# Tokens' 192 values as 128 and 64 rows in place of 96 and 96, the 64 rows of two outputs on the two halves of the array

## The chip, the cores and the metric

The program runs on one core of one Trainium2 chip, as one launch. The metric is the device time of that launch in microseconds (us). TensorE multiplies and transposes, VectorE (DVE), ScalarE (ACT) and GpSimd (POOL) work on what it leaves in the banks of PSUM, and SyncE (SP) issues most transfers. All data is float32.

## What is computed

The reference embeds 16 images (25 patches each) and 16 texts (77 words each) as 102 tokens of 192 values a sample, and passes them through four layers, each an attention and a feed-forward part with a normalisation ahead. The parts that matter here are these (the others, layer 0 and the two mixtures of experts, stay as they are):

```python
# layer 1, attention part: gated convolution, attention with 12 heads of 16, MLP
x = x + _ssm(_ln(x, ln1_g, ln1_b), in_proj_w, conv_w, conv_b, out_proj_w)      # x @ (192, 768)
a = _attn(_ln(x, ln2_g, ln2_b), qkv_w, qkv_b, H)                               # x @ (192, 576)
x = x + a @ attn_proj_w + attn_proj_b
h = jax.nn.gelu(_ln(x, ln3_g, ln3_b) @ ffn1_w + ffn1_b, approximate=False)     # x @ (192, 768)
x = x + h @ ffn2_w + ffn2_b
# layer 2: attention with 12 heads of 64, then an MLP
q = _split_heads(x @ w_q); k = _split_heads(x @ w_k); v = _split_heads(x @ w_v)  # each (192, 768)
h = jax.nn.gelu(jnp.einsum('td,hd->th', xt, in_weight) + in_bias, approximate=False)
# layer 3: attention without softmax, with a decay mask
qkv = x @ W_qkv + b_qkv                                                          # (192, 576)
```

Each product with x sums over its 192 values. An array of 128 rows does that in two steps.

## The kernel before

The 16 samples are worked on in four groups (NG) of four samples (GB): 408 tokens (TG) a group. Each engine has its own program, one `@block` each, and its order is the order in which the code is written. Semaphores tie the programs together. PSUM has eight banks: SBANKS are 0 and 1, TBANKS 2 and 3, OBANKS 4 and 5, XBANKS 6 and 7, FBANKS 2, 3, 6 and 7. In TensorE's program `claim` (L1541) waits until a bank is free, `filled` says that it is full, and `moved` waits until what is in it has been taken.

Six stages of layers 1 to 3 work alike, each in a loop over the four groups: the convolution (L1899), attention 1, MLP 1, attention 2, MLP 2 and attention 3. A group goes so:

1. DVE and POOL normalise the tokens into XN (token rows, 192 columns).
2. `xt` (L1590) turns XN with transposes at L1579: values 0 to 95 of the 408 tokens into one XBANK, values 96 to 191 into the other, each transpose a matmul with the identity of 102 columns. ACT copies both into XT, 96 rows by 2 parts (`turned`, L1330; L1338 with scale and bias in layer 1, L1336 without). TensorE waits for both copies.
3. `product` (L1557; its matmuls all bear L1561) makes each block of 128 outputs by 408 tokens in one bank from two matmuls over 96 rows each. There are 6 blocks in the convolution (first halves of the pairs to DVE, L1062 to L1066; second to ACT, L1470), 6 in attention 1 (q and k, ACT L1477 and L1484), 6 in an MLP (ACT L1345), 12 in attention 2 (ACT L1508 to L1513) and 4 blocks of 96 in attention 3. q and k use XBANKS alternately.
4. The values V are made with the tokens as rows: 102 by 192 for each sample in attention 1 and 3, two blocks of 102 by 384 for each sample in attention 2 (16 samples in all). DVE moves them out of OBANKS (L882, L885).
5. An attention stage then runs `attention`: scores (L1651) into SBANKS and bank 6, from which DVE takes the extremes (L847), ACT the exponentials (L1382), POOL the scaling (L620), TensorE the transposes (L1690) and the products with V (L1680), and the projection (L1663). An MLP makes its second product at L1627.

A float32 matmul is two records in the trace, each with its own load of weights. So a block of step 3 is 4 records, and 24 records are six blocks.

The mixtures of experts already have another layout: `first` (in `experts`) does two blocks with 128 rows each (L1993), and then the remaining 64 rows of both on the two halves of the array's rows (L1995).

SP loads the weights of layer 1 into AREA once layer 0 no longer reads it, with 22 transfers (W1_LOADS); POOL waits for them, spreads the weights of q and k into 32-row heads (L665), and gives `padded`, for which DVE waits at L1043 before its first normalisation of the stage. Those of layers 2 and 3 come with 15 transfers (W2_LOADS), ahead of the store of rows (L512) for the first mixture of experts.

## Time and profile before

| | us |
|---|---|
| median of 3 runs | 1974.52 |
| lowest and highest | 1970.76, 1977.46 |
| the profiled execution's own time | 1975.56 |
| its span, first to last instruction | 1973.8 |

The profile is of that one execution. It lists every instruction with its engine, line and tile, and tells for each idle time what ended it. A row of the timeline merges neighbours of one kind: start, length, how many (x), and in brackets how long the engine was idle before, and what ended that. The length reaches to the end of the last matmul's result, which lies after the start of the next row, so paces are taken here from start to start. The granted clock of TensorE is 1.00 at 2.4 GHz and 0.50 at 1.2 GHz.

### The profile page before, as it was taken

The numbers are of one execution on the slowest core, as the hardware profiler recorded it, in microseconds if no ns is written. First come the engines' busy times: TensorE is split into PE (matmuls) and PEld (weight loads), VectorE is DVE, ScalarE is ACT, GpSimd is POOL, SyncE is SP. The second block draws the span as 40 slices with busy tenths as digits, with TensorE's granted clock in tenths as the row PEclk, the third lists the DMA queues.
The fourth block names the chain that finished last, engine by engine and source line by source line (L and its number), as shares of the span: only waits on it lengthen the run. The fifth ranks groups of instructions, "written<-read, shape, count | busy, mean of one in ns | idle before, by whom it ended". The sixth has DMA issues, their size and how long they took to land.

```text
span 1973.8 us, 30712 instructions
## 1 busy us (share of the span) xinstructions
PE 1555.4 (79%) x9952; PEld 1118.0 (57%) x9952; DVE 746.1 (38%) x2156; ACT 653.9 (33%) x1667; POOL 382.8 (19%) x450
## 2 busy tenths in 40 slices
PE   7978788845554577788889589868999899789993
PEld 4555554634222244555567478736656677678883
DVE  1254535562111027655552612236543523531112
ACT  0455455511000013366653111124543532203331
POOL 5120211210000002222220135402211200023330
PEclk9587867766767678899999579979999999659997
DMA  7132141332999980000000535310000200134543
GB/s 191 31 92 81 40 121 31 91 97 67 273 286 283 285 248 31 1 1 0 0 0 0 152 108 175 118 39 1 0 0 0 96 0 0 34 94 149 161 139 87
DMA packets 85962, 177.79 MB, mean 90 GB/s; under 512 B 34602, under 2 KB 53200, under 8 KB 83832
## 3 DMA queue, kind: packets, MB, share of 16 engines
q1 hardware_dynamic: 71344, 127.50, 23.4%
q10 hardware_dynamic: 7392, 33.03, 5.7%
q0 software_dynamic: 7136, 16.10, 2.7%
q8 instruction: 51, 0.84, 0.2%
q14 instruction: 39, 0.32, 0.1%
HBM read 149.61 MB, written 26.99 MB: 89 GB/s over the span
## 4 chain that ended last, share of the span: by engine, by line
PE 51%; issue 16%; DMA 14%; DVE 14%; ACT 3%; POOL 1%; another core or an unknown queue 1%; SPq 0%; DVEq 0%; POOLq 0%; ACTq 0%
PE bank L1561 13%; DMA AREA<-in_fc 10%; PE bank L2005 6%; PE bank L1993 5%; PE bank L1995 4%; PE bank L1752 3%; PE bank L1663 3%; DVE MXU L847 3%; PE bank L1744 3%; DVE SMU L853 3%; PE bank L1651 2%; PE bank L1680 2%; PE bank L1806 2%; PE bank L1690 2%; PE bank L1961 1%
## 5 line engine op out<-in xcount | busy, mean ns | idle before, releaser
L1561 PE MATMUL bank<-XT,AREA 96*128 96x408 f32 (+1 forms) x640 | 241.2, 536 | 33.0 <-ACT XT L1338 15.7
L1561 PEld LDWEIGHTS bank<-XT,AREA 96*128 96x128 f32 (+1 forms) x640 | 122.6, 197 | 140.5 <-issue 101.4
L1651 PE MATMUL bank<-KZ,QT 128*102 128x102 f32 x1152 | 148.2, 271 | 6.9 <-ACT PB L1382 3.6
L620 POOL TENSOR_TENSOR PB<-PB,RCU 102x306 f32<-102x306 f32 x96 | 66.8, 696 | 390.4 <-DVE RCU L854 390.4
L1651 PEld LDWEIGHTS bank<-KZ,QT 128*102 128x102 f32 x1152 | 129.5, 184 | 22.3 <-issue 13.7
L606 POOL TENSOR_TENSOR RS<-VE,expo 102x4 f32<-102x4 f32 (+1 forms) x53 | 53.0, 1000 | 445.4 <-DVE VE L792 389.5
L2005 PE MATMUL bank<-WM,KZ 128*128 x660 | 120.4, 331 | 0.0
L1993 PE MATMUL bank<-KZ,SLOTS 128*128 128x128 f32 x660 | 116.0, 300 | 2.5 <-issue 2.5
L1663 PE MATMUL bank<-AREA,OT 128*102 128x192 f32 x384 | 89.8, 347 | 32.1 <-DVE SLOTS L1079 11.2
L1680 PE MATMUL bank<-PT,V 102*32 102x102 f32 (+1 forms) x1152 | 87.1, 274 | 28.2 <-DVE OT L868 28.2
L2005 PEld LDWEIGHTS bank<-WM,KZ 128*128 128x128 f32 x660 | 108.2, 194 | 0.4
L1993 PEld LDWEIGHTS bank<-KZ,SLOTS 128*128 128x128 f32 x660 | 93.4, 198 | 16.6 <-issue 5.3
L715 POOL DMA_INDIRECT rows_out<-KZ,TARGET x66 | 66.6, 1010 | 172.8 <-DVE KZ L1216 136.0
L1752 PE MATMUL bank<-AREA 64*102 64x203 f32 x384 | 86.5, 500 | 16.7 <-ACT SLOTS L1418 7.2
L1376 ACT ACTIVATE PT<-bank 102x306 f32<-102x306 f32 x192 | 81.4, 425 | 44.9 <-PE bank L1690 43.8
L1363 ACT ACTIVATE KZ<-bank,AREA 128x128 f32<-128x128 f32 x198 | 54.6, 374 | 119.1 <-PE bank L1995 62.0
L1209 DVE COPY KZ<-bank 128x256 f32<-128x256 f32 x66 | 28.0, 424 | 169.0 <-PE bank L1981 117.8
L1451 ACT ACTIVATE QT<-bank 128x512 f32<-128x512 f32 (+1 forms) x32 | 15.7, 490 | 221.5 <-PE bank L1806 221.5
L620 POOL TENSOR_TENSOR ON<-ON,RCU 102x306 f32<-102x306 f32 x96 | 66.8, 696 | 109.4 <-DVE RCU L854 109.4
L1995 PE MATMUL bank<-KZ,SLOTS 64*128 64x128 f32 x660 | 84.3, 333 | 0.0
L1017 DVE COPY QT<-bank 128x192 f32<-128x192 f32 x16 | 5.7, 358 | 206.6 <-PE bank L1806 206.6
L1752 PEld LDWEIGHTS bank<-AREA 64*102 64x102 f32 x384 | 60.5, 242 | 39.8 <-ACT SLOTS L1418 10.2
(292 smaller groups left out, 2722.4 us busy)
## 6 DMA issues: line engine op xcount, KB each, us to landing
WM<-in_fc SPq DMA_DIRECT2D x9, 2304.0 KB, 22.2
AREA<-in_fc SPq DMA_DIRECT2D x9, 2304.0 KB, 17.7
WM<-in_fc ACTq DMA_DIRECT2D x7, 2304.0 KB, 29.1
AREA<-in_fc ACTq DMA_DIRECT2D x7, 2304.0 KB, 28.3
SLOTS<-in_m3w SPq DMA_DIRECT2D x33, 384.0 KB
SLOTS<-in_m1w SPq DMA_DIRECT2D x33, 256.0 KB
AREA<-pos_scratch SPq DMA_DIRECT2D x16, 459.0 KB
pos_scratch<-AREA SPq DMA_DIRECT2D x8, 913.5 KB
```

The costliest lines, as they stand in the source:

```text
L620: pool.tensor_tensor(p, p, scale, ALU.mult).then_inc(sem["probs_ready"], 1)
L715: pool.indirect_dma_start(rows_out, bass.IndirectOffsetOnAxis(ap=TARGET[:, i:i + 1], axis=0), YO[i % YRING], None, bounds_check=2 * NB * T ...
L847: give(dve.tensor_reduce(MXU[:, n % 4, 0:HPU], scores, AX.X, ALU.min), "probs_in")
L1376: free(activation(PT[s % 2][:, 0:HPU, :], src, ACT.Copy), k)
L1561: last = pe.matmul(dst, lhsT, rhs, start=n == 0, stop=n == len(pieces) - 1)
L1651: last = pe.matmul(psum[k][0:T, cols(j)], QT[:, tile, cols(bb)], KALL[:, unit % per_tile * (HEADS // per_tile) + tile, cols(bb)], start=Tr ...
L1663: last = pe.matmul(psum[PROJBANK][0:T, 0:D], OT[bb % 2][:, m, :], wo[:, m, :], start=m == 0, stop=m == parts - 1)
L1680: last = pe.matmul(psum[k][row:row + rows, cols(tile)], by_head(dv)[:, bb * HEADS + h, :], PT[n % 2][:, j, :], start=True, stop=True)
L1752: last = pe.matmul(p[0:T, j * NREL:(j + 1) * NREL], head(QR, h, 2, 64, cols(bb)), head(RT, h, 2, 64, slice(0, NREL)), start=True, stop=True)
L1993: pe.matmul(p[:, c], w_all[:, (j * per + m) * 128:(j * per + m + 1) * 128], x[:, 0:TILE], start=True, stop=False)
L1995: both = [pe.matmul(p[:, c], w_half[64 * j:64 * j + 64, c], x[64 * j:64 * j + 64, TILE:2 * TILE], start=False, stop=True) for j, (k, p) in ...
L2005: last = pe.matmul(p[:, 0:D], HG[i % HRING][:, f * 128:(f + 1) * 128], w2[:, bass.ds(e, 1), f * D:(f + 1) * D].rearrange("p o d -> p (o d) ...
```

## The change

XT becomes XT2, 128 rows by 2 parts. Part 0 holds values 0 to 127. Part 1 holds values 128 to 191 twice: in rows 0 to 63 and again in rows 64 to 127. Weights are loaded accordingly: rows 0 to 127 of each matrix in one tile, and in a second tile (`...h`) rows 128 to 191 of every first output in partitions 0 to 63 and of every second output in partitions 64 to 127. The products of two outputs are made together (`twin`): two matmuls over 128 rows into two banks, then two over 64 rows, one on each half of the array's rows. `columns_twice` does so for blocks of outputs, `rows_twice` and a loop in attention 2 for V. The router's products keep the layout of 96 and 96 (XT is the first 96 rows of the same tile).

```diff
-W1_LOADS = 6 + 8 + 8
-W2_LOADS = 8 + 7
+W1_LOADS = 2 * 3 + 5 + 3 + 6 + 8 + 8
+W2_LOADS = 4 * 3 + 5 + 3 + 7
...
-        XT = sb("XT", [KD, 2, TG])
+        XT2 = sb("XT", [128, 2, TG])
+        XT = XT2[0:KD]
...
+            def load_split(full, half, src, name, columns):
+
+                load(full, t[src][0:128], name)
+                for j in range(2):
+                    load(half[64 * j:64 * j + 64], columns(t[src][128:D], j), name)
...
             step(pool.memset(wqk1, 0.0))
+            step(pool.memset(wqk1h, 0.0))
             pool.wait_ge(sem["w1_loaded"], 16 * W1_LOADS)
...
+            for full, _ in (g1, b1):
+                step(pool.tensor_copy(full[KD:128, :, 0], full[KD:128, :, 1]))
...
             with at.loop(act, NG) as g:
-                turned(XT, g1[:, 1, :], b1[:, 1, :])
-                for dst in range(3):
-                    k = at.bank(XBANKS)
-                    free(activation(QT[:, dst, :], full(k)[:, 0:TG], ACT.Identity, scale=-0.25,
-                                    bias=bqk1[:, dst:dst + 1]), k)
+                turned_split([g[:, 1, :] for g in g1], [b[:, 1, :] for b in b1])
                 for j in range(3):
-                    k = at.bank(XBANKS)
+                    k = at.bank(FBANKS)
+                    free(activation(QT[:, j, :], full(k)[:, 0:TG], ACT.Identity, scale=-0.25,
+                                    bias=bqk1[:, j:j + 1]), k)
+                    k = at.bank(FBANKS)
                     src = full(k)[:, 0:TG]
...
+            def xt_split(x=XN):
...
+                for part in range(2):
+                    k, p = claim(XBANKS)
+                    for bb in range(GB):
+                        if part == 0:
+                            last = pe.transpose(p[:, cols(bb)], x[:, bb, 0:128], ident[0:T, 0:T])
+                            continue
+                        pe.matmul(p[64:128, cols(bb)], x[:, bb, 128:D], ident[0:T, 0:T], start=True, stop=True)
+                        last = pe.transpose(p[0:64, cols(bb)], x[:, bb, 128:D], ident[0:T, 0:T])
+                    out.append(filled(last, k))
...
+            def twin(dsts, full, half):
+
+                for j, dst in enumerate(dsts):
+                    say_taken(pe.matmul(dst, *full(j), start=True, stop=False))
+                return [pe.matmul(dst, *half(j, slice(64 * j, 64 * j + 64)), start=False, stop=True)
+                        for j, dst in enumerate(dsts)]
...
-                for dst in range(6):
-                    k, p = claim(XBANKS)
-                    qk.append(filled(product(p[:, 0:TG], two(wqk1, dst * 128, (dst + 1) * 128)), k))
-                v_moved = pairs(lambda bb: token_rows(XT, bb, wqkv1, 2 * D, 3 * D))
-                moved(*qk[-2:])
+                qk = columns_twice(6, wqk1, wqk1h, apart=HPU)
+                v_moved = rows_twice(wqkv1[:, 2 * D:3 * D], wqkv1h[:, D:2 * D])
+                moved(*qk[-4:])
...
                 for bb in range(GB):
-                    for c in range(0, FF, 2 * D):
-                        k, p = claim(OBANKS)
-                        v_moved.append(filled(product(p[0:T, 0:2 * D], token_rows(XT, bb, wv2, c, c + 2 * D)), k))
-                moved(*qk[-2:])
-                attention(2, 64, wo2, v_moved[-2:])
+                    claims = [claim((OBANKS, SBANKS)[bb % 2]) for _ in range(2)]
+                    lasts = twin([p[0:T, 0:2 * D] for k, p in claims],
+                                 lambda j: (XT2[:, 0, cols(bb)], wv2[:, 2 * j * D:2 * (j + 1) * D]),
+                                 lambda j, r: (XT2[r, 1, cols(bb)], wv2h[r]))
+                    v_moved += [filled(last, k) for last, (k, p) in zip(lasts, claims)]
+                moved(*qk[-4:])
+                attention(2, 64, wo2, v_moved[-4:])
```

TensorE's order in one group of MLP 1, before. XN is the normalised input, AREA holds weights, KZ the hidden values; a size is output rows by columns.

```order
L1579 MATMUL bank6<-ident,XN 96x102 x4
L1544 REGISTER_ALU
L1579 MATMUL bank7<-ident,XN 96x102 x4
L1555 REGISTER_ALU
L1544 REGISTER_ALU
L1561 MATMUL bank2<-XT,AREA 128x408 x2
L1544 REGISTER_ALU
L1561 MATMUL bank3<-XT,AREA 128x408 x2
L1561 MATMUL bank6<-XT,AREA 128x408 x2
L1561 MATMUL bank7<-XT,AREA 128x408 x2
```

The same place now, to the end of the second pair of blocks.

```order
L1644 MATMUL bank6<-ident,XN 128x102 x4
L1590 REGISTER_ALU
L1646 MATMUL bank7<-ident,XN 64x102
L1647 MATMUL bank7<-ident,XN 64x102
...
L1655 MATMUL bank2<-XT,AREA 128x408
L1655 MATMUL bank3<-XT,AREA 128x408
L1656 MATMUL bank2<-XT,AREA 128x408
L1656 MATMUL bank3<-XT,AREA 128x408
L1655 MATMUL bank6<-XT,AREA 128x408
L1655 MATMUL bank7<-XT,AREA 128x408
L1656 MATMUL bank6<-XT,AREA 128x408
L1656 MATMUL bank7<-XT,AREA 128x408
```

The second part of XT takes eight matmuls (L1646 and L1647, four times each) in place of four, and each pair of banks is filled by four matmuls (L1655 over 128 rows, L1656 over 64 rows) whose last two end together.

TensorE's order where attention 2 goes from V to the scores, now (before, V used banks 4 and 5 alone and each bank was filled by two matmuls in a row).

```order
L1655 MATMUL bank0<-AREA,XT 102x384
L1655 MATMUL bank1<-AREA,XT 102x384
L1656 MATMUL bank0<-AREA,XT 102x384
L1656 MATMUL bank1<-AREA,XT 102x384
L1601 REGISTER_ALU x3
L1732 REGISTER_ALU
L1737 MATMUL bank0<-KZ,QT 102x102 x3
```

The last V of a group now lies in banks 0 and 1, and the first scores go into bank 0, so they wait until DVE has taken V out of it.

SP's order at the loads of layer 1, before and then now: 22 transfers up to `in_qk_b`, then 36.

```order
L414 DMA AREA<-in_in_proj 96x2x768
L414 DMA AREA<-in_out_proj 128x3x192
L414 DMA AREA<-in_qkv 96x2x576
L414 DMA AREA<-in_proj 128x576
L414 DMA AREA<-in_ffn 96x2x768
```

```order
L416 DMA AREA<-in_in_proj 128x768
L416 DMA AREA<-in_in_proj 64x384 x2
L416 DMA AREA<-in_qkv 128x576
L416 DMA AREA<-in_qkv 64x192 x4
L416 DMA AREA<-in_ffn 128x768
L416 DMA AREA<-in_ffn 64x3x128 x2
```

Each matrix of 192 rows is now three transfers or more in place of one.

## Rows read from the trace of the kernel before

**Rows 1.** The page, part 4: the chain that ended last, by engine.

```profile
PE 51%; issue 16%; DMA 14%; DVE 14%; ACT 3%; POOL 1%; another core or an unknown queue 1%; SPq 0%; DVEq 0%; POOLq 0%; ACTq 0%
```

**Rows 2.** Stretches (convolution, attention 2): length, busy us and counts, clock, DMA.

```profile
745.00:824.00 79.00, 61.21 (x224) 40.56 (x224) 55.32 (x142) 27.84 (x40) 24.46 (x21) 0.86 0.00 1
...
1302.00:1565.00 263.00, 241.85 (x1499) 165.02 (x1498) 130.71 (x332) 120.74 (x340) 48.58 (x68) 0.99 0.00 0
```

**Rows 3.** Timeline, TensorE, one group of MLP 2 (granted clock 1.00).

```profile
1584.65 8.48 PE L1561 MATMUL bank<-XT,AREA 96*128 96x408 f32 x24 [0.83 <-ACT XT L1336]
1592.97 8.00 PE L1627 MATMUL bank<-AREA,KZ 128*102 128x192 f32 x48
1600.81 0.86 PE L1579 MATMUL bank<-ident,XN 102*96 102x102 f32 x8
```

**Rows 4.** Timeline, TensorE: the experts' pairs, and layer 0's heads on half the rows.

```profile
1884.61 0.71 PE L1993 MATMUL bank<-KZ,SLOTS 128*128 128x128 f32 x4
1885.26 0.49 PE L1995 MATMUL bank<-KZ,SLOTS 64*128 64x128 f32 x4
1885.68 0.71 PE L1993 MATMUL bank<-KZ,SLOTS 128*128 128x128 f32 x4
...
192.07 0.94 PE L1752 MATMUL bank<-AREA 64*102 64x203 f32 x8
```

**Rows 5.** Timeline, TensorE, attention 2: three heads of 64 columns.

```profile
1339.23 0.56 PE L1680 MATMUL bank<-PT,V 102*64 102x102 f32 x6
```

**Rows 6.** Timeline, ACT: the copies into XT, in MLP 2 and in MLP 1.

```profile
1583.51 0.90 ACT L1336 ACTIVATE XT<-bank 96x408 f32<-96x408 f32 x2 [6.29 <-PE bank L1579]
...
1031.60 1.26 ACT L1338 ACTIVATE XT<-bank,AREA 96x408 f32<-96x408 f32 x2 [6.29 <-PE bank L1579]
```

**Rows 7.** Timeline, attention 2 from V to the scores: TensorE, then DVE.

```profile
1322.69 10.48 PE L1561 MATMUL bank<-AREA,XT 96*102 96x384 f32 x32
1333.01 1.78 PE L1651 MATMUL bank<-KZ,QT 128*102 128x102 f32 x18
...
1333.28 0.56 DVE L882 COPY V<-bank 102x384 f32<-102x384 f32 x1 [0.73 <-PE bank L1561]
1333.96 1.07 DVE L847 TENSOR_REDUCE MXU<-bank 102x3 f32<-102x306 f32 x2
```

**Rows 8.** Timeline, attention 1, the second group: TensorE, ACT, then DVE.

```profile
877.08 7.09 PE L1561 MATMUL bank<-XT,AREA 96*128 96x408 f32 x20 [1.05 <-ACT XT L1338]
...
886.77 2.77 PE L1561 MATMUL bank<-AREA,XT 96*102 96x192 f32 x16
890.20 1.83 PE L1651 MATMUL bank<-KZ,QT 128*102 128x102 f32 x18 [0.67 <-issue]
...
882.83 7.26 ACT L1484 ACTIVATE KZ<-bank,AREA 32x408 f32<-32x408 f32 x12 [0.77 <-PE bank L1561]
...
890.99 1.07 DVE L847 TENSOR_REDUCE MXU<-bank 102x3 f32<-102x306 f32 x2 [0.80 <-PE bank L1651]
```

**Rows 9.** Timeline, the convolution's third group: TensorE, then DVE.

```profile
791.63 5.80 PE L1561 MATMUL bank<-XT,AREA 96*128 96x408 f32 x8 [3.99 <-DVE marked L761]
...
794.76 0.70 DVE L1062 TENSOR_SCALAR KZ<-bank,AREA 128x408 f32<-128x408 f32 x1 [0.57 <-PE bank L1561]
```

**Rows 10.** Timeline, the loads of layer 1: SP, POOL and DVE.

```profile
720.26 0.32 SPq L414 DMA_DIRECT2D AREA<-in_in_proj  x1
...
730.22 4.04 SPq L414 DMA_DIRECT2D AREA<-in_qk_b  x8
...
736.24 1.23 POOL L665 COPY AREA<-AREA 96x192 f32<-96x192 f32 x4 [14.64 <-DMA AREA<-in_qk_b]
...
740.00 0.17 DVE L1043 TENSOR_SCALAR AREA<-AREA 128x3 f32<-128x3 f32 x1
```

**Rows 11.** Timeline, SP: the store of rows, and its next issue.

```profile
1101.51 8.48 SPq L512 DMA_DIRECT2D rows_in<-V  x16
1123.88 0.37 SPq L526 DMA_DIRECT2D SLOTS<-in_m1w  x1
```

More of the change, by code:

```diff
@@ L315, in build @@
         a2(KD, 2, NB * T)
-        wq2, wk2, wv2 = a2(KD, 2, FF), a2(KD, 2, FF), a2(KD, 2, FF)
+        wq2, wk2, wv2, wi2 = (a2(128, FF) for _ in range(4))
+        wq2h, wk2h, wv2h, wi2h = (a2(128, FF // 2) for _ in range(4))
         wo2, bo2 = a2(128, 6, D), a2(T, D)
-        wi2, bi2, wu2 = a2(KD, 2, FF), a2(128, FT), a2(128, FT, D)
-        wqkv3, bqk3, bv3 = a2(KD, 2, 3 * D), a2(KD, 4), a2(T, D)
+        bi2, wu2 = a2(128, FT), a2(128, FT, D)
+        wqkv3, wqkv3h, bqk3, bv3 = a2(128, 3 * D), a2(128, 2 * D), a2(KD, 4), a2(T, D)
         decay = a2(T, T)
@@ L877, in values @@
                 v5 = by_head(dv)
-                for first in range(0, GB * HEADS, per):
-                    k = at.bank(OBANKS)
+                for n, first in enumerate(range(0, GB * HEADS, per)):
+                    k = at.bank((OBANKS, SBANKS)[n // 2 % 2])
                     src = full(k)[0:T, 0:per * dv].rearrange("p (h d) -> p h d", d=dv)
@@ L1339, in turned, with turned_split @@
                                         bias=bias[:, part:part + 1]), k)
+            def turned_split(scale=None, bias=None):
+                for part in range(2):
+                    k = at.bank(XBANKS)
+                    src = full(k)[:, 0:TG]
+                    if scale is None:
+                        free(activation(XT2[:, part, :], src, ACT.Copy), k)
+                    else:
+                        free(activation(XT2[:, part, :], src, ACT.Identity, scale=scale[part][:, part:part + 1],
+                                        bias=bias[part][:, part:part + 1]), k)
             def hidden(tiles, func, bias, src_ready=None):
@@ L1612, in pairs, with mlp @@
                 return out
-            def mlp(tiles, w1, x, w2):
-                tokens = []
-                for m in range(tiles):
-                    k, p = claim(FBANKS)
-                    last = product(p[:, 0:TG], [(w1[:, part, m * 128:(m + 1) * 128], x(part)) for part in range(2)])
-                    tokens.append(filled(last, k))
+            def mlp(tiles, w1, w2):
+                tokens = columns_twice(tiles, *w1)
                 for first in range(0, GB, 2):
@@ L1900, in convolution_in @@
                 at.first_banks()
-                xt()
+                xt_split()
                 for c in range(CT3):
-                    k, p = claim(SBANKS)
-                    filled(product(p[:, 0:TG], two(win1, c * 128, (c + 1) * 128)), k)
-                    k, p = claim(TBANKS)
-                    filled(product(p[:, 0:TG], two(win1, INNER + c * 128, INNER + (c + 1) * 128)), k)
+                    at_c = c * 128
+                    claims = claim(SBANKS), claim(TBANKS)
+                    lasts = twin([p[:, 0:TG] for k, p in claims],
+                                 lambda j: (win1[:, j * INNER + at_c:j * INNER + at_c + 128], XT2[:, 0, :]),
+                                 lambda j, r: (win1h[r, at_c:at_c + 128], XT2[r, 1, :]))
+                    for last, (k, p) in zip(lasts, claims):
+                        filled(last, k)
             def convolution_out(place):
```

123 lines of the change are left out of this document (80 added, 43 removed).

## The prediction

> **What bounds the kernel now.** I read the chain that ended last first: TensorE has 51% of it, and 16% is time in which TensorE waits for nothing that the profile shows [rows 1]. The stretches come next, one for each stage. Attention 2 has TensorE busy for 242 of 263 us at a granted clock of 0.99, while in the convolution it is busy for 61 of 79 us, beside DVE's 55, at 0.86 [rows 2]. So TensorE's time is the time of the kernel in the dense stages, and in the convolution it is so only in part. The timeline of a dense stage shows how full: one group of MLP 2 runs from transposes to transposes with a single wait, 0.83 us for the copies into XT [rows 3].
>
> **A price for a matmul.** 24 records of 408 columns take 8.32 us from start to start (1584.65 to 1592.97), of which the first load of weights is about 0.1; that leaves 0.342 us a record. 48 records of 192 columns take 7.84 us, 0.163 each [rows 3]. Both are 0.85 ns a column, whether 96 or 128 rows are used. V of attention 2, 384 columns, has 0.322 us (10.32 / 32) [rows 7]. So rows cost nothing and records do: a pair of blocks is now 8 records, 8 x 0.342 = 2.74 us.
>
> **Do the halves run at once, and what does going to halves cost?** The experts' pairs show it. One unit there is four records over 128 rows and four over 64 rows, and repeats after 1.07 us (1884.61 to 1885.68) [rows 4]. At 0.85 ns a column, 128 columns are 0.109 us; eight in a row would be 0.87 and six (the halves at once) 0.65. That the halves do overlap is shown by the other row: eight records of 203 columns on half the rows, four into one bank and four into the next, take 0.94 us with everything that follows the last one [rows 4], where eight in a row would be 8 x 0.173 = 1.38 us before that. So the unit is 6 x 0.109 plus two changes between whole and halved rows, and a change costs (1.07 - 0.65) / 2 = 0.21 us: the array runs empty, and the next load of weights lies bare.
>
> A pair of blocks then costs 6 x 0.342 + 2 x 0.21 = 2.47 us, **0.27 less than now**. More than half of the two saved records (0.68) goes back in changes. For V: 8 x 0.322 = 2.58 becomes 6 x 0.322 + 0.38 (102 columns load faster, so 0.19 a change) = 2.31, 0.27 less for a sample of attention 2; 8 x 0.163 = 1.30 becomes 0.98 + 0.38 = 1.36, 0.06 more for two samples of attention 1 and 3.
>
> **XT.** The second part takes eight matmuls for four, those of rows 64 to 127 as plain matmuls of two records. On two column halves they can overlap: three heads of 64 columns, two of them on one half, take 0.56 us for six records [rows 5]. A record of 102 columns is 0.087, and the last result needs 0.16 to come out (1584.65 + 8.48 is 0.16 past the next start [rows 3]), so 0.56 is a load of 0.05, four records in a row (0.35) and 0.16; six in a row would be 0.73. So part 1 is 8 x 0.087 = 0.70, a change of 0.15 (64 columns load in half the time) and 0.08 for the wider part 0, against 0.35 now: its bank is full 0.58 us later. ACT's copies hide a part. Without bias the second copy starts 0.40 after the first (0.90 for both), and its bank is full just before; 0.5 is late. With bias it starts 0.6 later (1.26 for both) [rows 6], so 0.31 is late. Were the eight to run in a row (12 records), it would be 0.34 more each.
>
> **Stage by stage**, four groups each:
> - MLP 1: 3 pairs save 0.81, XT adds 0.31: -2.0 us. MLP 2: 0.81 less 0.5: -1.2. Cover for the last pair, whose banks are now full together: ACT takes 0.6 us for 408 columns (7.26 / 12 [rows 8]), and TensorE wants them after 8 and 10 records of 0.163, 1.3 and 1.6 us on; enough.
> - Attention 2: 6 pairs save 1.62, V saves 1.06, XT adds 0.5. A wait is added: the first scores go into bank 0, which holds V until DVE has copied it. Now DVE starts on the first scores (L847) at 1333.96, 0.95 after the last V record (1333.01) [rows 7]; its own last copy ends only then. In the changed order DVE starts a copy 0.27 after V's end, as now (1333.28), frees bank 0 after 0.56 more, the six records take 0.1 to be released, 0.09 to load and 6 x 0.09, and DVE is there 0.25 after: 1.8 after V's end. That is 0.85 later, and behind it stand the exponentials, POOL and all else, since TensorE waits for them at once. Net -1.33 a group: -5.3 us.
> - Attention 1 is bound by ACT at this point. Its twelve copies of k run without a gap from 882.83 for 7.26 us, and the scores start when they end (890.20), 13.0 after the first product (877.2); DVE at 890.99 [rows 8]. The changed order alternates q and k, so ACT has a k to copy after the first pair: 2.42 + 3 x (0.6 + 2.43) = 11.6 after the first product. TensorE's pairs and V (3 x 2.47 + 0.5 for a bank + 2 x 1.36 = 10.6) and DVE's two moves of V after them (0.6 each, to 12.0) stay below DVE's new start of 12.4. So the stall shrinks by 1.36, XT adds 0.31: -4.2 us.
> - Attention 3: two pairs save 0.54, V adds 0.12, XT 0.5: +0.3.
> - Convolution: TensorE waits 3.99 for DVE, then DVE 0.57 for TensorE at block 5 [rows 9]. DVE's block used to be full after 4 records, and is now full after the whole pair. At full clock that is 0.9 us later (2.26 for 1.37), cold 1.8. I followed the four groups: +1.5 in the first (cold), the third gives back what TensorE saves, the last ends about 2 later. I take +2, from -1 to +5.
> - Loads of layer 1: 36 for 22. The eight small ones are issued every 0.46 us (4.04 / 8 with the first longer), the 22 take 14.1 us to 734.3, of which 10.1 is issuing and 3.9 waits on full queues. 36 x 0.46 = 16.6, up to 20.5 with the same waits: 2.5 to 6.5 later. DVE starts at 740.00, 2.5 us after POOL's copies end (737.47) [rows 10]. POOL's own work grows by 0.25. So 0.2 to 4.2 is late; I take 1.5. Layers 2 and 3: 12 more loads stand ahead of the store of rows, +5.5 us; SP sits idle from 1109.98 to 1123.88 after it [rows 11], so nothing.
>
> The **sum**: -2.0 - 1.2 - 5.3 - 4.2 + 0.3 + 2 + 1.5 = -8.9 us. The profiled execution took 1975.6, so 1966.7; that execution lies 1.0 above the median of 1974.5, hence 1965.6, rounded to 1966.
>
> **Rivals.**
> 1. A change costs more behind 408 columns than behind 128. There are 160 changes in the pairs and 64 in V, 224 in all; each 0.04 us more eats the gain, and at 0.28 in place of 0.21 the time is 1966 + 16 = 1982, **slower than before**. It decides at 0.25. For it: a 408-column record runs on for 0.16 us after its last column, and nothing shows a change right behind one in a full-clock stretch. Against: the experts' 128-column records run on as long, and their change does not wait for it.
> 2. The halves do not overlap in this order (both records of one, then both of the other), so that a pair has seven record times. This adds 80 x 0.342 and 16 x 0.163 + 16 x 0.322, 35 us: about 2001. Against it stands the 0.94 us row of [rows 4], which has this very order.
>    [...]
> 3. XT's part 1 runs in a row (24 x 0.34 = +8), or the convolution and the loads come out at their upper ends (+3, +2.7): 1972 to 1977, no change to be told.
> 4. The waits hide less than I think: the scores of attention 2 start earlier, and the convolution and loads cost nothing (-3.4, -2, -1.5): 1959. It is inside the forecast's sign.
>
> **How the numbers follow.** About 0.3% (5.9 us) is what a measurement of this kernel can tell from no change. The forecast with rival 4 (1957 to 1971): 0.67, of which 0.05 lies within 0.3%. Rival 3: 0.19, nearly all within. Rival 1: 0.10, of which 0.02 within. Rival 2: 0.04. That is faster 0.62, same 0.25, slower 0.13. The range leaves out rival 2, the worse half of rival 1 and the best tail: 1955 to 1978.
>
> **What would show it.** In the trace after: pairs that repeat every 2.47 us in MLP 2, with the halves of two banks starting within 0.02 us of each other; a group of MLP 2 of 17.5 us for 17.85; the first DVE extreme of attention 2 1.8 us after V; q and k copies of attention 1 alternating, the scores at 11.6 us; the first L1043 at 740.2 to 744 us. Wrong would be: a pair above 2.74 us, a granted clock that falls in the dense stages because the changes leave TensorE idle, or part 1 of XT above 1.1 us.

## The result, and the profile after

The changed kernel takes **1999.55 us** (median of 4 runs, 1988.78 to 2011.26), the kernel before 1972.64 us (median of 4, 1969.08 to 1977.46). The ratio is 1.0136, with a 95% interval from 1.0073 to 1.0199: slower, where the forecast was 1966 us and faster. The profiled execution took 2002.3 us with a span of 2000.3; before, the span was 1973.8. All rows below are of these two executions unless another kernel is named.

The chain that ended last looks as before [rows 1], a little more of it in `issue` (the page, part 4, of the changed kernel):

```profile
PE 49%; issue 17%; DVE 14%; DMA 13%; ACT 4%; SPq 1%; POOL 1%; DVEq 0%; POOLq 0%; ACTq 0%
```

The place to look at is one group of MLP 2, the stage whose group had a single wait before [rows 3]. Timeline of TensorE, changed kernel (start, duration, engine, line, output<-inputs, count, idle time before). L1644 makes part 0 of XT; L1646 (matmuls to rows 64:128) and L1647 (transposes to rows 0:64) make part 1; L1655 are the products over 128 rows (whole), L1656 those over 64 rows (halves); L1713 is the MLP's second product:

```profile
1593.96 0.51 PE L1644 MATMUL bank<-ident,XN 102*128 102x102 f32 x4
1594.41 0.39 PE L1646 MATMUL bank<-ident,XN 102*64 102x102 f32 x2
1594.73 0.28 PE L1647 MATMUL bank<-ident,XN 102*64 102x102 f32 x1
1594.93 0.39 PE L1646 MATMUL bank<-ident,XN 102*64 102x102 f32 x2
...
1596.31 0.28 PE L1647 MATMUL bank<-ident,XN 102*64 102x102 f32 x1
1597.49 2.68 PE L1655 MATMUL bank<-XT,AREA 128*128 128x408 f32 x4 [0.90 <-ACT XT L1383]
1600.10 1.55 PE L1656 MATMUL bank<-XT,AREA 64*128 64x408 f32 x4
1601.58 1.64 PE L1655 MATMUL bank<-XT,AREA 128*128 128x408 f32 x4
1603.15 0.96 PE L1656 MATMUL bank<-XT,AREA 64*128 64x408 f32 x4
1604.03 1.64 PE L1655 MATMUL bank<-XT,AREA 128*128 128x408 f32 x4
...
1606.49 8.09 PE L1713 MATMUL bank<-AREA,KZ 128*102 128x192 f32 x48
```

Three things stand there. The second pair starts at 1601.58 and the third at 1604.03: **2.45 us a pair**, as the prediction has it (2.47). XT takes from 1593.96 to 1596.58, **2.62 us where it was 0.86** [rows 3], because matmuls and transposes of 64 columns take turns, one couple for each sample ("to and fro" from here on), 0.52 us a couple (1594.41 to 1594.93). And the first pair takes 4.09 us (1597.49 to 1601.58), not 2.45. The stretches of the same group say why (length, then busy us and counts of PE, PE's loads, DVE, ACT, POOL, then the granted clock, DMA share and GB/s):

```profile
1593.90:1596.60 2.70, 2.69 (x18) 1.55 (x16) 1.76 (x6) 0.51 (x1) 0.00 (x0) 1.00 0.00 0
1597.40:1601.50 4.10, 4.01 (x8) 1.47 (x8) 1.25 (x4) 1.03 (x1) 1.01 (x1) 0.58 0.00 0
1601.60:1606.40 4.80, 4.80 (x18) 1.94 (x16) 0.00 (x0) 2.18 (x4) 0.00 (x0) 1.00 0.00 0
```

The granted clock was 0.58 in the first pair: TensorE was at its lower level, 1.2 GHz, for most of it, and back at 2.4 GHz for the next. Before it lay the to and fro and 0.90 us of waiting. A first pair of 3.9 to 4.1 us stands in eight groups (two of attention 1, one of MLP 1, three of MLP 2, two of attention 3) in which the kernel before kept its full clock.

By stages, from the first transposes of one stage to those of the next (us; "change" and the last column are differences to before; the last column is of experiment 7 below, in which one word of the change is different):

| | before | after | change | predicted | two matmuls |
|---|---|---|---|---|---|
| start of the convolution | 747.2 | 749.2 | +2.0 | +1.5 | +1.5 |
| convolution | 77.5 | 79.4 | +1.9 | +2 | -0.8 |
| attention 1 | 188.1 | 191.4 | +3.3 | -4.2 | -6.5 |
| MLP 1 | 72.8 | 76.9 | +4.1 | -2.0 | -2.5 |
| attention 2 | 264.3 | 262.7 | -1.6 | -5.3 | -7.4 |
| MLP 2 | 71.4 | 80.1 | +8.7 | -1.2 | -1.3 |
| attention 3 | 53.4 | 62.2 | +8.8 | +0.3 | +0.4 |

The stages between and behind them, which the change does not touch, move by about 1 us or less. The start of the convolution holds more than the loads: DVE comes to its wait there 1.6 us earlier than in the kernel before (742.01 less 3.57 against 740.00), so +2.0 is a wait of 3.6 less 1.6 that the traced executions differ by ahead of it.

The waits that the prediction spoke of, in the changed kernel. Attention 2: TensorE's last halves of V and first scores, then DVE's last copy of V and its first look at the scores; attention 1, second group: first products, ACT's second and third block of k, first scores; layer 1's loads: SP, POOL, DVE:

```profile
1407.46 0.89 PE L1656 MATMUL bank<-AREA,XT 64*102 64x384 f32 x4
1409.07 1.92 PE L1737 MATMUL bank<-KZ,QT 128*102 128x102 f32 x18 [0.71 <-DVE V L918]
...
1408.45 1.15 DVE L918 COPY V<-bank 102x384 f32<-102x384 f32 x2 [1.14 <-PE bank L1656]
1409.89 1.07 DVE L883 TENSOR_REDUCE MXU<-bank 102x3 f32<-102x306 f32 x2 [0.28 <-PE bank L1737]
...
882.59 1.63 PE L1655 MATMUL bank<-XT,AREA 128*128 128x408 f32 x4 [1.06 <-ACT XT L1385]
893.90 1.86 PE L1737 MATMUL bank<-KZ,QT 128*102 128x102 f32 x18 [0.64 <-ACT KZ L1530]
...
733.95 5.11 SPq L416 DMA_DIRECT2D AREA<-in_qk_b  x8
...
740.48 0.43 POOL L694 COPY AREA<-AREA 32x3 f32<-32x3 f32 x2 [20.66 <-DMA AREA<-in_qk_b]
...
742.01 0.17 DVE L1079 TENSOR_SCALAR AREA<-AREA 128x3 f32<-128x3 f32 x1 [3.57 <-POOL AREA L701]
```

### The profile page after: what moved, and what is told of

Same layout as the page of the kernel before. It is cut to its first block, busy times and chain, and to the rows that moved or that the text cites. A ratio compares the mean times of both kernels' runs of the same rounds, so it can differ in the third digit from the quotient of the medians.

```text
span 2000.3 us, 31192 instructions
## 1 busy us (share of the span) xinstructions
PE 1567.0 (78%) x10144; PEld 1075.6 (54%) x10144; DVE 745.9 (37%) x2156; ACT 649.8 (32%) x1667; POOL 382.7 (19%) x452
## 4 chain that ended last, share of the span: by engine, by line
PE 49%; issue 17%; DVE 14%; DMA 13%; ACT 4%; SPq 1%; POOL 1%; DVEq 0%; POOLq 0%; ACTq 0%
DMA AREA<-in_fc 9%; PE bank L2091 5%; PE bank L2079 5%; PE bank L1655 5%; PE bank L2081 4%; PE bank L1607 3%; PE bank L1838 3%; PE bank L1749 3%; PE bank L1737 3%; DVE MXU L883 3%; DVE SMU L889 3%; PE bank L1656 3%; PE bank L1830 2%; PE bank L1892 2%; PE bank L1766 2%
## 5 line engine op out<-in xcount | busy, mean ns | idle before, releaser
L1655 PE MATMUL bank<-XT,AREA 128*128 128x408 f32 (+1 forms) x320 | 147.5, 588 | 30.5 <-ACT XT L1383 10.6
L1655 PEld LDWEIGHTS bank<-XT,AREA 128*128 128x128 f32 (+1 forms) x320 | 58.6, 204 | 101.3 <-issue 86.6
L2079 PEld LDWEIGHTS bank<-KZ,SLOTS 128*128 128x128 f32 x660 | 93.6, 198 | 16.6 <-issue 5.4
L1838 PE MATMUL bank<-AREA 64*102 64x203 f32 x384 | 80.7, 463 | 19.9 <-ACT SLOTS L1465 8.7
L1656 PE MATMUL bank<-XT,AREA 64*128 64x408 f32 (+1 forms) x320 | 83.1, 599 | 0.0
```

The source lines that it names most:

```text
L1655: say_taken(pe.matmul(dst, *full(j), start=True, stop=False))
L1656: return [pe.matmul(dst, *half(j, slice(64 * j, 64 * j + 64)), start=False, stop=True) for j, dst in enumerate(dsts)]
L1838: last = pe.matmul(p[0:T, j * NREL:(j + 1) * NREL], head(QR, h, 2, 64, cols(bb)), head(RT, h, 2, 64, slice(0, NREL)), start=True, stop=True)
L2079: pe.matmul(p[:, c], w_all[:, (j * per + m) * 128:(j * per + m + 1) * 128], x[:, 0:TILE], start=True, stop=False)
```

## The experiments

Three theories stood after the trace. **A**: the loss is XT's part 1, by its own length and by the clock that falls behind it. **B**: the clock falls for the split products. **C**: the pairs, their new order or the loads cost what is lost. Every ratio is to the kernel before on the same chip; the medians of that kernel lie between 1962 and 1977 us from chip to chip, so ratios are what can be compared. Rows and spans are of one traced execution of each kernel.

**1. Part 1 by overwriting.** Four whole transposes of values 64 to 191 put the 64 values on rows 64:128, four narrow ones then write rows 0:64 again.

```diff
+                        last = pe.transpose(p[:, cols(bb)], x[:, bb, 64:D], ident[0:T, 0:T])
+                    for bb in range(GB if part else 0):
                         last = pe.transpose(p[0:64, cols(bb)], x[:, bb, 128:D], ident[0:T, 0:T])
-                        pe.matmul(p[64:128, cols(bb)], x[:, bb, 128:D], ident[0:T, 0:T], start=True, stop=True)
```

> XT's part 1 is made by four full-width transposes of values 64 to 191 (they leave the 64 values in rows 64:128) and four narrow ones that then write values 128 to 191 over rows 0:64; nothing else differs from the changed kernel. Theory A (the loss is the turning: 16 groups of records that go to and fro between the array's column halves, 2.62 us of transposes a group where 0.86 stood, and the granted clock that falls after it): transposes 1.35 us a group (12 records of 0.086 and two changes), 24 groups x -1.27 = -30.5 us, and the slow first pairs (4.09 in place of 2.45 us in 8 groups) go, -13: about 1956 us, faster than the kernel before. Theory B (the clock falls for the split products themselves): the transposes come down but the slow first pairs stay: about 1969. Theory C (the split products or the added loads are what costs): the time stays within 10 us of the changed kernel's 1999.6.

Measured: 1957.05 us, ratio 0.9915 (0.9876 to 0.9955). TensorE, a group of MLP 2:

```profile
1584.96 0.52 PE L1644 MATMUL bank<-ident,XN 102*128 102x102 f32 x4
1585.31 0.51 PE L1646 MATMUL bank<-ident,XN 102*128 102x102 f32 x4
1585.66 0.51 PE L1648 MATMUL bank<-ident,XN 102*64 102x102 f32 x4
1587.05 1.63 PE L1656 MATMUL bank<-XT,AREA 128*128 128x408 f32 x4 [0.87 <-ACT XT L1383]
...
1589.50 1.64 PE L1656 MATMUL bank<-XT,AREA 128*128 128x408 f32 x4
```

The transposes take 1.22 us, the first pair 2.45 (1587.05 to 1589.50), and none of the eight slow first pairs is left. The pairs, their order and the loads are those of the changed kernel. A holds, B and C fall.

**2. The same records in another order**: the four matmuls first, then the four transposes.

```diff
-                        pe.matmul(p[64:128, cols(bb)], x[:, bb, 128:D], ident[0:T, 0:T], start=True, stop=True)
+                        last = pe.matmul(p[64:128, cols(bb)], x[:, bb, 128:D], ident[0:T, 0:T], start=True, stop=True)
+                    for bb in range(GB if part else 0):
                         last = pe.transpose(p[0:64, cols(bb)], x[:, bb, 128:D], ident[0:T, 0:T])
```

> The changed kernel with the same records in XT's part 1 in another order: the four matmuls to rows 64:128 first, then the four transposes to rows 0:64. Theory A1 (the price is the change from one column half to the other, 8 a group): 12 records of 0.086 and two changes, transposes 1.8 us a group in place of 2.62, -20 us, and the slow first pairs mostly go: 1967 to 1980 us. Theory A2 (each record on half of the columns is slow by itself, 0.18 us): transposes stay at 2.6 us a group and the time at 2000.

Measured: 1967.97 us, ratio 0.9972 (0.9938 to 1.0005).

```profile
1590.45 0.51 PE L1644 MATMUL bank<-ident,XN 102*128 102x102 f32 x4
1590.89 0.91 PE L1646 MATMUL bank<-ident,XN 102*64 102x102 f32 x8
1591.74 0.54 PE L1648 MATMUL bank<-ident,XN 102*64 102x102 f32 x4
```

All transposes of the group take 1.83 us in place of 2.62, with the same twelve records in part 1. Inside a block they are 0.087 us apart now. So a narrow record is not slow by itself; six changes more between the two kinds cost 0.79 us a group, 0.13 each. The slow first pairs are gone here too.

**3. Each output alone**, on top of experiment 1: whole, half, whole, half.

```diff
-                for j, dst in enumerate(dsts):
-                    say_taken(pe.matmul(dst, *full(j), start=True, stop=False))
-                return [pe.matmul(dst, *half(j, slice(64 * j, 64 * j + 64)), start=False, stop=True)
-                        for j, dst in enumerate(dsts)]
+                lasts = []
+                for j, dst in enumerate(dsts):
+                    say_taken(pe.matmul(dst, *full(j), start=True, stop=False))
+                    lasts.append(pe.matmul(dst, *half(j, slice(64 * j, 64 * j + 64)), start=False, stop=True))
+                return lasts
```

> As the run with the overwritten part 1, but each output's half product stands right behind its own full one, so that no two halves stand side by side. Theory: a pair of 408 columns then takes 8 records of 0.342 and four changes of 0.1, 3.14 us in place of 2.45; 80 such pairs +55 us, 16 V pairs of 384 columns +10, 16 of 192 columns +5: some 70 us above its partner, about 2026. Rival (the two halves of an adjacent pair do not share time, or their sharing is hidden behind other waits): within 15 us of its partner.

Measured: 2110.61 us, ratio 1.0682 (1.0602 to 1.0763). TensorE in MLP 2, then the stretch of attention 2's first group:

```profile
1719.92 0.95 PE L1657 MATMUL bank<-XT,AREA 128*128 128x408 f32 x2 [0.92 <-ACT XT L1383]
1720.80 0.95 PE L1658 MATMUL bank<-XT,AREA 64*128 64x408 f32 x2
...
1723.44 0.95 PE L1657 MATMUL bank<-XT,AREA 128*128 128x408 f32 x2
```

```profile
1352.00:1457.00 105.00, 99.76 (x376) 47.95 (x377) 34.81 (x87) 30.50 (x85) 12.17 (x17) 0.66 0.00 1
```

A pair takes 3.52 us (1719.92 to 1723.44): eight records of 0.342 are 2.74, and four changes cost 0.2 each. My expectation had 0.1 a change, which was wrong; the prediction's 0.21 was right. The rest above the 86 us of the 80 pairs is V, and the clock: the first group of attention 2 took 105 us at a granted 0.66, the next one 73. Halves side by side are what the change lives on: without them it is 1.07 us worse in each pair.

**4. The to and fro in the kernel before**, as dead work behind its own transposes.

```diff
+                    for bb in range(GB if extra and part else 0):
+                        pe.matmul(p[64:128, TG:TG + T], src[:, bb, 128:D], ident[0:T, 0:T], start=True, stop=True)
+                        last = pe.transpose(p[0:64, TG:TG + T], src[:, bb, 128:D], ident[0:T, 0:T])
```

> The kernel before, with its 96 and 96 rows, its products and its loads, and behind the transposes of XT's part 1 the to and fro of the changed kernel as dead work (four matmuls to rows 64:128 and four transposes to rows 0:64 of columns that nobody reads). Theory A (the turning costs 2.1 us a group and it alone brings the granted clock down): +50 us and slow first products in some of the MLPs' and attention's groups, up to +13: 2023 to 2036 us. Theory B (the clock falls for the split products): +50 us, 2023, with the clock at 1.00 in both MLPs.

Measured: 2032.05 us, ratio 1.0266 (1.0180 to 1.0353), so +53. The two MLPs, which had a granted clock of 1.00 before:

```profile
1030.00:1117.00 87.00, 82.48 (x379) 60.30 (x377) 23.50 (x77) 28.91 (x39) 4.04 (x4) 0.94 0.00 0
1609.00:1692.00 83.00, 79.89 (x370) 58.62 (x369) 16.49 (x68) 27.46 (x39) 4.03 (x4) 0.96 0.15 57
```

With the old products, of 96 and 96 rows, the clock falls behind the to and fro, in seven groups (four of the MLPs, two of attention 2, one of the convolution): theory B falls for a second time.

**5 and 6. Is it the to and fro, or the wait behind it as well?** First the changed kernel with ten useless whole transposes in the wait, then the changed kernel with part 1 waited for ahead of the halves only, so that two whole products run in the wait.

```diff
+                if filler:
+                    spare.append([claim(FBANKS) for _ in range(2)])
+                    for n in range(10):
+                        pe.transpose(spare[0][0][1][:, cols(n % GB)], x[:, n % GB, 0:128], ident[0:T, 0:T])
                 moved(*out)
...
-                    claims = [claim(FBANKS) for _ in range(2)]
+                    claims = spare.pop() if spare else [claim(FBANKS) for _ in range(2)]
...
-                xt_split()
+                xt_split(filler=False)
```

> The changed kernel itself, with ten full-width transposes of no use (0.09 us each) in the 0.87 us that TensorE idles behind XT's transposes, in all stages but the convolution; they write a bank that the next product overwrites. Theory (the granted clock falls for low activity, the to and fro and the idle time together): the slow first pairs (4.09 us in place of 2.45, 8 groups) go, -13, and the filler costs up to 0.2 us a group: 1987 to 1991. Rival (the to and fro alone brings the clock down, or the split products): the slow pairs stay, 2000 to 2004.

```diff
-                moved(*out)
+                moved(out[0])
+                pending[:] = [out[1]]
...
+                moved(*pending)
+                pending.clear()
                 return [pe.matmul(dst, *half(j, slice(64 * j, 64 * j + 64)), start=False, stop=True)
```

> The changed kernel with its to and fro as it is; XT's part 1 is waited for ahead of the halves only, so that both whole products of the first pair run in the 0.87 us that TensorE idled. Theory (the idle time behind the to and fro is part of what brings the clock down): 24 x -0.85 = -20 us, and the slow first pairs (4.09 in place of 2.45 us in 8 groups) go as well, -13: 1966 us, a ratio of 0.997 to the kernel before. Rival (the to and fro alone brings the clock down): -20 and the slow pairs stay: 1980, 1.003.

Measured: 1975.91 us with the useless transposes, ratio 1.0070 (1.0033 to 1.0106), and 1961.84 us with the products, ratio 0.9931 (0.9904 to 0.9959). One group of MLP 2 with useless transposes (L1654), the stretches of both MLPs in that kernel, then one group with early products:

```profile
1579.80 0.28 PE L1649 MATMUL bank<-ident,XN 102*64 102x102 f32 x1
1579.91 1.04 PE L1654 MATMUL bank<-ident,XN 102*128 102x102 f32 x10
1580.78 1.59 PE L1661 MATMUL bank<-XT,AREA 128*128 128x408 f32 x4
...
1583.19 1.64 PE L1661 MATMUL bank<-XT,AREA 128*128 128x408 f32 x4
```

```profile
1006.00:1081.00 75.00, 75.00 (x394) 52.81 (x393) 22.24 (x74) 27.60 (x39) 4.03 (x4) 1.00 0.00 0
1559.00:1633.00 74.00, 74.00 (x393) 52.49 (x392) 16.48 (x68) 26.15 (x39) 4.03 (x4) 1.00 0.17 64
```

```profile
1585.91 1.56 PE L1658 MATMUL bank<-XT,AREA 128*128 128x408 f32 x4
1587.40 0.95 PE L1661 MATMUL bank<-XT,AREA 64*128 64x408 f32 x4
1588.29 1.64 PE L1658 MATMUL bank<-XT,AREA 128*128 128x408 f32 x4
```

In both the to and fro is as long as in the changed kernel, and in both the first pair takes 2.4 us (1580.78 to 1583.19, 1585.91 to 1588.29) and none of the eight slow first pairs is left. So in these kernels the clock falls only where an idle 0.6 to 1.1 us follows the to and fro. In the convolution, where no useless work was put in, the third group's first pair fell in that same kernel (4.01 us; 2.42 in the changed kernel), so which groups are hit is not fixed. The useless work alone brings the ratio down by 0.66 points, 13 us, as much as the eight slow pairs. The intervals of the two ratios overlap, so this share rests on the traces: the five stages with useless transposes are 17 us shorter there, 13 of them in the first pairs.

**7. One word: a matmul for the transpose.** My reading of [rows 5] was that two column halves run at once. There both kinds are matmuls; in the change one is a transpose.

```diff
-                        last = pe.transpose(p[0:64, cols(bb)], x[:, bb, 128:D], ident[0:T, 0:T])
+                        last = pe.matmul(p[0:64, cols(bb)], x[:, bb, 128:D], ident[0:T, 0:T], start=True, stop=True)
```

> The changed kernel with one word changed: the narrow transposes to rows 0:64 of XT's part 1 are plain matmuls with the identity, two records each, as those to rows 64:128 are. That is four records more a group. Theory (a transpose and a matmul can't share the array, two matmuls on different column halves can, as the heads of attention 2 show, whose records start 7 ns apart): each couple takes two record times, part 1 takes 0.7 us and two changes, the transposes 1.4 to 1.5 us a group in place of 2.62, 24 x -1.15 = -28, and the slow first pairs go, -13: about 1959, a ratio of 0.993. Rival (column halves do not share time here, whatever the kind): 16 records in a row, the transposes stay above 1.9 us, and with eight changes above 2.6 us: 0.999 to 1.02.

Measured: 1959.80 us, ratio 0.9925 (0.9888 to 0.9962).

```profile
1602.85 0.30 PE L1646 MATMUL bank<-ident,XN 102*64 102x102 f32 x1
1602.86 0.30 PE L1647 MATMUL bank<-ident,XN 102*64 102x102 f32 x1
1602.99 0.25 PE L1646 MATMUL bank<-ident,XN 102*64 102x102 f32 x1
1602.99 0.25 PE L1647 MATMUL bank<-ident,XN 102*64 102x102 f32 x1
...
1603.52 0.25 PE L1647 MATMUL bank<-ident,XN 102*64 102x102 f32 x1
1604.65 1.63 PE L1655 MATMUL bank<-XT,AREA 128*128 128x408 f32 x4 [0.88 <-ACT XT L1383]
```

Sixteen records for twelve, and part 1 takes 0.9 us (1602.85 to 1603.77) where it took 2.2: the records of the two halves start 7 ns apart. None of the eight slow first pairs is left. This is the experiment that settles the case: banks, rows, values and order are the same, and only the kind of one instruction differs. The kernel that I had priced is this one, and its stages stand beside the prediction in the table above. Its span is 16.6 us shorter than before, where 8.9 was forecast; the forecast's own ratio, 0.9957, lies inside the interval.

**8. Halves next to halves.** Four experiments ask what the split can give. On top of experiment 1, every second pair goes half, half, whole, whole, so that halves stand next to halves:

```diff
+                step = [False, True] if turn[0] else [True, False]
+                turn[0] = not turn[0]
+                for n, whole in enumerate(step):
...
+                        pieces = full(j) if whole else half(j, slice(64 * j, 64 * j + 64))
+                        lasts.append(pe.matmul(dst, *pieces, start=n == 0, stop=n == 1))
```

> As the run with the overwritten part 1 (1957 us), with every second pair in the order half, half, full, full, so that the halves of one pair stand next to those of the following one. Theory (a change between whole and halved rows costs 0.2 us, as 3.52 us for a pair one by one against 2.45 says: two changes more, and two records more of 0.342): changes a group fall from 6 to 4 in the convolution and the MLPs, 10 to 6 in attention 1, 20 to 10 in attention 2, 8 to 4 in attention 3: 24 fewer in one group of each stage, 96 in all, -19 us: 1938. Rival (the 0.2 us belong to the first weights of every half product, whatever stood before): less than 5 us.

Measured: 1930.42 us, ratio 0.9823 (0.9776 to 0.9870), 18 us below experiment 1 by the ratios: 96 changes fewer by 0.2 us are 19, so a change is worth its 0.2 us wherever it is avoided.

**9. No narrow transposes.** XT in two overlapping parts, values 0 to 127 and 64 to 191, each made by whole transposes. An even output takes part 0 whole and part 1's rows 64:128, an odd one part 1 whole and part 0's rows 0:64:

```diff
+                        last = pe.transpose(p[:, cols(bb)], x[:, bb, 64 * part:64 * part + 128], ident[0:T, 0:T])
...
-                                 lambda j: (w[:, (m + j * apart) * width:(m + j * apart + 1) * width], XT2[:, 0, :]),
-                                 lambda j, r: (half[r, i * width:(i + 1) * width], XT2[r, 1, :]))
+                                 lambda j: (w[:, (m + j * apart) * width:(m + j * apart + 1) * width], XT2[:, j, :]),
+                                 lambda j, r: (half[r, i * width:(i + 1) * width], XT2[r, 1 - j, :]))
```

> As the alternating kernel, with XT in two full-width parts, values 0 to 127 and 64 to 191: an even output takes part 0 whole and the last 64 values from rows 64:128 of part 1, an odd one part 1 whole and the first 64 values from rows 0:64 of part 0; no narrow transposes are left, and 12 loads more are issued (5 in layer 1, 7 in layer 2). Theory: transposes 0.86 us a group as in the kernel before in place of 1.21, 24 x 0.35 = -8: 1930. Rival (loads on the sync engine's queue set the start of layer 1): at most a few us of it are left.

Measured: 1926.59 us, ratio 0.9815 (0.9763 to 0.9867). The interval is too wide to show a difference from its partner. In the trace the transposes are back to 0.86 us, but with bias the wait for ACT's two copies grows from 0.92 to 1.15 us and takes 0.23 of the 0.35; the span is 4.7 us shorter. The expectation missed that ACT is next in line.

**10. The first product early.** It waits for part 0 alone:

```diff
-                moved(*out)
+                moved(out[0])
+                pending[:] = [out[1]]
...
+                        if j == 1:
+                            moved(*pending)
+                            pending.clear()
```

> As the one with overlapping parts; the first product waits for part 0's copy alone, the copy of part 1 is waited for ahead of the second. Theory (TensorE idles 0.87 us a group for the copies of XT): the first product starts 1.3 us after the first transpose in place of 1.7, 24 x 0.45 = -11: 1919. Rival (the idle time only moves to the second product, or to ScalarE's copies of the filled banks): within 4 us of its partner.

Measured: 1917.72 us, ratio 0.9765 (0.9726 to 0.9804). The interval overlaps that of experiment 9; the span is 10.7 us shorter, and the wait behind the transposes of MLP 2 falls from 0.93 to 0.42 us. One group of MLP 2 now takes 16.16 us, where it took 17.85 [rows 3]:

```profile
1569.10 0.86 PE L1651 MATMUL bank<-ident,XN 102*128 102x102 f32 x8
1570.38 7.03 PE L1671 MATMUL bank<-XT,AREA 128*128 128x408 f32 x24 [0.42 <-ACT XT L1391]
1577.34 8.08 PE L1730 MATMUL bank<-AREA,KZ 128*102 128x192 f32 x48
1585.26 0.86 PE L1651 MATMUL bank<-ident,XN 102*128 102x102 f32 x8
```

**11. Fewer loads.** In this kernel the convolution's start is late: DVE waits for POOL's small copies, which wait for the last of 41 loads. One tensor of 128 x 18 for layer 1's scales, shifts and biases makes it 26:

```diff
-            for (full, half), name in ((g1, "ln_g"), (b1, "ln_b")):
...
+            load(vec1, t["vec1"], "w1_loaded")
...
-                    load(bqk1[32 * u:32 * u + 16, 3 * q:3 * q + 3], t["qk1_b"][q, u], "w1_loaded")
```

> The fastest kernel so far, with layer 1's scales, shifts and q and k biases laid out beforehand as one tensor of 128 x 18: 1 load in place of 16, 26 in place of 41, and GpSimd's four small copies gone. Theory (VectorE waits 6.5 us for GpSimd's copies, which wait for the last of the loads, issued every 0.46 us): 15 x 0.46 = 6.9 us of issuing less, the wait is gone, -6 us, a ratio of 0.973 to the kernel before. Rival (the wait is for the large loads' data, not for the issuing): the wait stays above 3 us and the time within 3 us of its partner.

Measured: 1910.44 us, ratio 0.9721 (0.9664 to 0.9778), the fastest kernel here. DVE at that place, in the kernel with 41 loads and in the one with 26:

```profile
738.80 0.17 DVE L1087 TENSOR_SCALAR AREA<-AREA 128x3 f32<-128x3 f32 x1 [6.54 <-POOL AREA L709]
```

```profile
726.78 0.17 DVE L1079 TENSOR_SCALAR AREA<-AREA 128x3 f32<-128x3 f32 x1 [1.30 <-POOL AREA L701]
```

The wait falls by 5.2 us and below 3, which speaks for the issuing. About 1.0 of it is POOL's four small copies, which are gone too (736.79 to 737.76). POOL now starts 6.4 us after the last load was issued (719.35 to 725.73), where it was 2.5 (734.27 to 736.79), so the data of the loads counts as well. The intervals of the two kernels overlap, so the gain itself rests on this row; in the eight kernels here with 36 loads the same wait was 0.7 to 3.6 us.

**12. How much of that does the split deserve?** The kernel before, with its 96 and 96 rows, and the first product waiting for part 0 alone:

```diff
                 for n, (lhsT, rhs) in enumerate(pieces):
+                    if n == 1:
+                        late_part()
...
-                moved(*turn_group(x, part_of))
+                first, second = turn_group(x, part_of)
+                moved(first)
+                pending[:] = [second]
```

> The kernel before, 96 and 96 rows, with one thing of the fastest kernel: the first product of the same six stages waits for XT's part 0 alone, part 1's copy is waited for between the two matmuls of that product. Theory: TensorE's idle time behind the transposes falls from 0.69 to 1.19 us a group to about 0.45, 24 x -0.45 = -11 us, a ratio of 0.9945 to the kernel before; what the fastest kernel (0.9765) gained above that, some 1.8% or 35 us, is then the split's own. Rival (most of the fastest kernel's gain is this wait): 0.985 or below.

Measured: 1961.75 us, ratio 0.9927 (0.9898 to 0.9956). The ratio of experiment 10 is 0.9765: of its 2.35 points, 0.7 are this wait, and some 1.6 points, 32 us give or take 10 by the two intervals, the split with its overlapping parts and its alternating order.

## Why the prediction was wrong

**The step that failed is XT.** The prediction read [rows 5] as column halves that run at once, and carried it over to a matmul beside a transpose: part 1 is "8 x 0.087 = 0.70", its bank full 0.58 us later. With two matmuls that is nearly so: experiment 7 has 1.37 us of transposes for 0.86, 0.51 more. With a transpose it is 1.76 more. One couple in the changed kernel has three records 0.14, 0.18 and 0.21 us apart in place of 0.087 each, and nothing overlaps. Part 1 takes 2.2 us, twice the 1.1 that the prediction had named as a sign of being wrong. Rival 3 saw the row of twelve but priced it without the changes, at 0.34 us on top, where 1.2 came on top; so its 1972 to 1977 was too low as well. Beside this stands a rule of the Trainium skill that I did not weigh ("TensorEngine Tiling (Array Packing)", Restrictions and Gotchas): column tiling excludes the transpose mode for FP32 input. The trace agrees in that no transpose shares time with a narrow matmul, and each change between the two costs 0.13 us (experiment 2). That this rule is the cause is not shown.

**What it cost.** Transposes and the wait behind them, against what the prediction added: MLP 2 3.50 us for 1.69, +1.81 where +0.5 was put down; by the same rows 1.45 too little in attention 1, 1.2 in MLP 1, 1.45 in attention 2 and 1.45 in attention 3. Four groups each, that is 27 us, priced at full clock; in the first groups of attention 1 and 2, at the lower clock, it is 2.9 us more than before and not 1.8 or 1.9.

**The clock.** The prediction named a granted clock that falls in the dense stages as a sign of error, but priced it nowhere and looked for it in the pairs. It fell behind XT, in eight groups, 1.5 to 1.64 us each: 13 us. Experiments 1 and 2 keep the idle time, experiments 5 and 6 keep the to and fro, and neither alone brings it down. 27 and 13 are 40; the sum was wrong by 35.4 (-8.9 for +26.5 between the spans), so the other steps came out 5 better.

**The other steps, one by one.**
- *A price for a matmul and for a change*: right. Pairs of 2.45 us for 2.47; a change 0.2 (experiment 3) for 0.21. Rival 1, a change of 0.28 behind 408 columns, falls.
- *The halves run at once*: right, they start 7 ns apart in the pairs too, and rival 2 falls, though its 2001 us is nearly the time that was measured. That closeness is chance: a number that fits is no evidence for its mechanism.
- *V and the scores of attention 2*: DVE turns to the scores at 1409.89, 1.54 us after V's last result (1407.46 + 0.89); counted so it was 0.79 before [rows 7], so 0.75 is added where 0.85 was predicted. Without XT's share the group gained 2.3 (65.27 to 64.91, with XT's +1.95), predicted 1.83.
- *q and k of attention 1*: scores 11.3 us after the first product (882.59 to 893.90), where it was 13.1 [rows 8]; predicted 11.6, though the sum that stands there gives 11.5.
- *Convolution*: +1.9, predicted +2; but in experiment 7 it is -0.8, so some of what was measured belongs to XT and the clock, and the agreement is partly luck.
- *Loads of layer 1*: DVE waits 3.57 us for POOL where it waited for nothing [rows 10]. It is within the 0.2 to 4.2 of the prediction, and above the 1.5 taken. In the eight kernels with these 36 loads the wait was 0.7 to 3.6 us, one trace each, so the +2.0 for +1.5 in the table is partly luck.
- *Attention 3 and the MLPs*: in experiment 7 +0.4, -2.5 and -1.3, predicted +0.3, -2.0 and -1.2.
- *The first groups of attention 1 and 2*: not priced apart. In experiment 7 they gain 2.9 and 2.7 us, with TensorE at its lower clock at their start; the groups behind them gain 1.2 and 1.5 to 1.6, near the 1.05 and 1.33 predicted. Attention 1 and 2 come out 2.3 and 2.1 us better than forecast there, the convolution 2.8, and I have not traced what makes the last.

So XT, and the clock behind it, is the step that turned the sign. It was carried from a row whose instructions were all of one kind. The other terms of the dense stages held at full clock; the convolution missed by 2.8 us to the good side, which is luck.

## What to carry to other kernels

Before two things are put down as running side by side, look whether the row that shows it has both of the same kind: a narrow matmul and a narrow transpose took turns at 0.52 us a couple where two matmuls took 0.17, and doing more records, all of one kind, was faster. Where row or column halves are used, put halves next to halves, in alternating order if need be, since each change takes 0.2 us of the 0.68 that a pair saves. Such a to and fro ahead of a wait can bring the clock down behind it, so put work into the wait: two whole products that had to be done anyway gave back the wait's time and the clock (experiment 6).

## What the runs showed of the hardware

- **A float32 transpose did not share the array with a matmul on the other column half**; two matmuls did. Four samples: 2.2 us to and fro (changed kernel), 1.4 us in two blocks (experiment 2), 0.9 us as sixteen matmul records (experiment 7).
- **The clock fell behind transposes with a to and fro in them, followed by a wait of 0.9 to 1.1 us**: in 8 of the 20 groups of the changed kernel whose transposes, 2.6 us, ran at full clock with no longer wait behind them. With 1.8 us of transposes in blocks and the same waits (experiment 2) it fell in none of these, nor where the wait was filled, even with useless transposes (granted 1.00 in both MLPs). In the kernel before with the same to and fro as dead work (3.0 us of transposes, waits of 0.6 to 1.0 us, experiment 4) it fell in 7.
- **A change between whole and halved rows costs 0.2 us at full clock**, behind 408 columns as behind 128: a pair takes 3.52 us with four changes and none side by side, 2.45 with two. It costs this in either direction: from 1601.58 to 1603.15 are four whole records, 1.37, and 0.20; from 1603.15 to 1604.03 are two record times, 0.68, and 0.20. In alternating order the three pairs of an MLP take 6.96 us, in the order of the change 7.35. The Trainium skill ("TensorEngine Tiling (Array Packing)", Tiling Modes, Key Properties) says that a change of the tiling mode, not of the tile alone, drains TensorE; the trace agrees, and puts the price to it.
